# Attention stage: projections of two sequences one slot later, a tile's sum ahead of the next tile's gathers, statistics between row maxima

## The reference

```python
x = layernorm(x + ssm(x))             # state-space mixer
x = layernorm(x + moe(x))             # 64 experts, 8 per token, and a shared one
x = layernorm(x + attention(x))       # 16 heads of 8, per sequence
x = layernorm(x + mlp(x))             # three layers of +1/-1 weights
```

```python
q = split_heads(x @ Wq.T + bq)
k = split_heads(x @ Wk.T + bk)
v = split_heads(x @ Wv.T + bv)
scores = einsum('hbnd,hbmd->hbnm', k, q) * SCALE
attn = softmax(scores, axis=-1)
out = einsum('hbnm,hbmd->hbnd', attn, v)
```

## Time and profile before

| | us |
|---|---|
| three runs, median (lowest to highest) | 871.92 (866.49 to 875.07) |
| the profiled execution | 876.69 |
| its span, first to last instruction | 874.9 |
| mean granted TensorE clock | 0.85 of full speed |
| PE busy | 618.2 (71%) |
| DVE busy | 483.3 (55%) |
| ACT busy | 400.1 (46%) |
| POOL busy | 365.7 (42%) |

### The profile page before, as it was taken

How to read it: one execution, slowest core, us unless ns; L and a number is a source line. 1 busy time by engine, 2 the same in 40 slices (tenths; PEclk the granted TensorE clock), 3 DMA queues, 4 the chain that set the end, 5 groups by cost and what they waited for, 6 DMA issues and landing times.

```text
span 874.9 us, 13107 instructions
## 1 busy us (share of the span) xinstructions
PE 618.2 (71%) x3680; PEld 385.2 (44%) x3713; DVE 483.3 (55%) x1238; ACT 400.1 (46%) x900; POOL 365.7 (42%) x401
## 2 busy tenths in 40 slices
PE   4872109600179999930978977877978999998995
PEld 2451006300158999920968863222222233343443
DVE  4870015300036655600645677686866887867986
ACT  4420103200024666600534648555756777787651
POOL 4157750677720000075032433787477070013552
PEclk9876558855579999965879997898989999999999
DMA  8999410211102666631545645242241131000001
GB/s 270 373 247 344 169 42 1 87 54 51 48 1 72 178 172 171 180 88 42 159 119 145 166 126 150 62 138 56 52 127 54 29 104 56 1 2 0 2 12 37
DMA packets 99628, 91.52 MB, mean 105 GB/s; under 512 B 10784, under 2 KB 84608, under 8 KB 98688
## 3 DMA queue, kind: packets, MB, share of 16 engines
q1 hardware_dynamic: 90704, 75.01, 28.6%
q0 software_dynamic: 7680, 15.74, 6.2%
q10 hardware_dynamic: 1200, 0.23, 0.1%
HBM read 45.14 MB, written 45.61 MB: 104 GB/s over the span
## 4 chain that ended last, share of the span: by engine, by line
PE 46%; another core or an unknown queue 18%; DVE 14%; issue 12%; ACT 6%; DMA 2%; POOL 1%; ACTq 1%; SPq 0%; POOLq 0%; DVEq 0%
PE ps L1621 7%; PE ps L1608 6%; PE ps L1726 5%; PE ps L1736 5%; PE ps L1716 4%; DVE mx L1230 4%; PE ps L1631 3%; PE ps L1616 3%; PE ps L1530 2%; PE ps L1535 2%; ACT big L807 2%; DVE arena L1348 1%; ACT arena L773 1%; DMA dmat_s<-dmat 1%
## 5 line engine op out<-in xcount | busy, mean ns | idle before, releaser
L1230 DVE TENSOR_REDUCE mx<-ps 128x2 f32<-128x1024 f32 x128 | 151.0, 1217 | 49.5 <-PE ps L1716 37.9
L807 ACT ACTIVATE big<-ps 128x512 f32<-128x512 f32 x256 | 141.4, 598 | 67.2 <-PE ps L1726 32.7
L558 POOL DMA_INDIRECT big<-od,idx x72 | 69.0, 958 | 187.2 <-DMA od<-big 123.6
L542 POOL DMA_INDIRECT xd<-xt,idx x120 | 116.2, 968 | 69.7 <-issue 35.7
L1535 PE MATMUL ps<-arena,hmT 96*128 96x128 f32 x128 | 26.9, 343 | 125.8 <-issue 102.1
L1152 DVE TENSOR_TENSOR hm<-sg,ps 128x176 f32<-128x176 f32 x124 | 41.7, 336 | 118.1 <-ACT sg L745 74.1
L1621 PE MATMUL ps<-arena,xbT 128*128 x496 | 99.8, 325 | 4.7 <-DVE xbT L1156 2.7
L1726 PE MATMUL ps<-arena 128*128 128x512 bf16 (+1 forms) x234 | 82.6, 395 | 24.4 <-ACT big L807 11.6
L1608 PE MATMUL ps<-arena,hmT 96*128 x496 | 80.4, 286 | 26.4 <-issue 22.4
L1535 PEld LDWEIGHTS ps<-arena,hmT 96*128 96x128 f32 x128 | 21.0, 229 | 142.2 <-issue 108.0
L735 ACT ACTIVATE big<-ps 128x256 f32<-128x256 f32 x124 | 47.7, 384 | 76.2 <-PE ps L1608 47.0
(11 more groups left out here) (221 smaller groups left out, 1088.7 us busy)
## 6 DMA issues: line engine op xcount, KB each, us to landing
big<-xd SPq DMA_DIRECT2D x62, 256.0 KB
od<-big SPq DMA_DIRECT2D x62, 256.0 KB
arena<-scr SPq DMA_DIRECT2D x96, 96.0 KB
xd<-zeros SPq DMA_DIRECT2D x1, 8192.0 KB
xd<-zeros SPq DMA_DIRECT2D x1, 7680.0 KB, 30.9
arena<-w_gu SPq DMA_DIRECT2D x4, 1408.0 KB, 21.3
arena<-w_d SPq DMA_DIRECT2D x4, 768.0 KB, 17.7
scr<-places SPq DMA_DIRECT2D x8, 384.0 KB
```

The lines of the kernel that those rows point to most:

```text
L542: pool.indirect_dma_start(out=xd[f], out_offset=bass.IndirectOffsetOnAxis(ap=idx[:, t, k:k + 1], axis=0), in_=xt[:, t], in_offset=None).th ...
L558: pool.indirect_dma_start(out=slot[:, k], out_offset=None, in_=od[f], in_offset=bass.IndirectOffsetOnAxis(ap=idx[:, t, k:k + 1], axis=0)). ...
L807: act.activation(ering[:, HG * (mt % 2) + h], ps[:, 4 + h % 2, :], ACT.Exp, scale=SCALE).then_inc(exp_ready, 1)
L1230: v.tensor_reduce(mx[:, k, TB * h + 2 * a:TB * h + 2 * a + 2], ps[:, 2 * a:2 * a + 2, :], AX_X, ALU.max).then_inc(s1_free, 1)
```

## The change

Sequence 1 stays as it was. For sequence 2 (and 3):

- x goes from slot 0 to slot 1 of group 4 (8), q from slot 1 to slot 2, k from slot 2 to slot 0 of group 5 (9), v from slot 0 to slot 1 of that group.
- The normalisation comes behind the third maximum of group 4 (fourth of group 8), the v bias behind the seventh maximum of group 5 (9). DVE's split steps of sequence 2 have places of their own: q behind the seventh and eighth maximum of group 4 and the first of group 5, k behind the fourth, fifth and sixth of group 5.
- The statistics of sequence 3 go from the end of group 7 to behind the second maximum of group 8; those of sequence 2 stay at the end of group 3.
- SP writes the keys of sequences 2 and 3 behind the maxima's DMA and not in front of it.
- POOL sums tile 11 ahead of tile 12's gathers, and makes the root of sequence 2 behind four gathers of tile 12 and not behind two of tile 13.

```diff
--- before.py
+++ after.py
@@ -75,12 +75,15 @@
 
 
     LATER = {(0, 0): ("x", 1), (0, 1): ("q", 1), (0, 2): ("k", 1), (1, 0): ("v", 1),
-             (4, 0): ("x", 2), (4, 1): ("q", 2), (4, 2): ("k", 2), (5, 0): ("v", 2),
-             (8, 0): ("x", 3), (8, 1): ("q", 3), (8, 2): ("k", 3), (9, 0): ("v", 3)}
+             (4, 1): ("x", 2), (4, 2): ("q", 2), (5, 0): ("k", 2), (5, 1): ("v", 2),
+             (8, 1): ("x", 3), (8, 2): ("q", 3), (9, 0): ("k", 3), (9, 1): ("v", 3)}
     SLOTS = ((1, 2), (2, 2), (3, 0))
-    STATS_IN = {4: 2, 8: 3}
-    TURN_IN = {i: b for (i, _), (what, b) in LATER.items() if what == "x"}
-    PARTS_AT = ((0, 2, 1), (0, 3, 0), (0, 3, 1), (0, 3, 1), (1, 0, 0), (1, 0, 1))
+    STATS_AT = {(3, HG - 1, 1): 2, (8, 0, 1): 3}
+    NORM_AT = {(4, 1, 0): 2, (8, 1, 1): 3}
+    V_AT = {(1, 2, 0): 1, (5, 3, 0): 2, (9, 3, 0): 3}
+    PARTS_AT = {1: ((0, 2, 1), (0, 3, 0), (0, 3, 1), (0, 3, 1), (1, 0, 0), (1, 0, 1)),
+                2: ((4, 3, 0), (4, 3, 1), (5, 0, 0), (5, 1, 1), (5, 2, 0), (5, 2, 1))}
+    WRITE_KEYS_LATER = (6, 10)
     WRITE_IN = {2: 1, 6: 2, 10: 3}
     HEAD_GROUPS = 10
     LOADS = {0: (2,), 1: (3,), 2: (4, 5), 3: (6,), 4: (7,), 6: (8, 9), 7: (10,), 8: (11,), 10: (12, 13), 11: (14,), 12: (15,)}
@@ -445,12 +448,15 @@
                 if i in WRITE_IN:
                     write_parts(sp, WRITE_IN[i], 0)
                     load_stack(sp, GB * WRITE_IN[i], 0)
-                    write_parts(sp, WRITE_IN[i], 1)
+                    if i not in WRITE_KEYS_LATER:
+                        write_parts(sp, WRITE_IN[i], 1)
                 sp.wait_ge(mT_copied, i + 1)
                 hd = HG * (i % (2 * GB))
                 if i >= 1:
                     sp.wait_ge(max_in, 16 * i)
                 sp.dma_start(kst[KM:P, hd:hd + HG, :].rearrange("p h n -> p (h n)"), mT[:, i % 2, :]).then_inc(max_in, 16)
+                if i in WRITE_KEYS_LATER:
+                    write_parts(sp, WRITE_IN[i], 1)
                 for n in LOADS.get(i, ()):
                     if n % GB:
                         load_stack(sp, n, 0)
@@ -594,11 +600,14 @@
             bring(1, FIRST[1], back_slot(FIRST[1]))
             rstd_of(2 * B + 1)
             for t in range(FIRST[1] + 1, NT):
-                bring(1, t, back_slot(t), 0, 2)
-                if t == 3 * TB + 1:
+                if t == 3 * TB:
+                    sum_rows(t - 1)
+                bring(1, t, back_slot(t), 0, 4)
+                if t == 3 * TB:
                     rstd_of(2 * B + 2)
-                bring(1, t, back_slot(t), 2, TOP_K)
-                sum_rows(t - 1)
+                bring(1, t, back_slot(t), 4, TOP_K)
+                if t != 3 * TB:
+                    sum_rows(t - 1)
             sum_rows(NT - 1)
 
             def qk_parts(b):
@@ -1266,6 +1275,11 @@
                     v.wait_ge(s_r, 3 * i + 3)
                     v.tensor_tensor(mp[:, k, 2], r, mp[:, k, 1], ALU.subtract).then_inc(split_done, 1)
 
+            def late_stats(b):
+
+                v.wait_ge(summed, TB * (b + 1) - MINE - DENSE)
+                stats(tmp, B + b)
+
             def dve_group(i, k):
                 ahead = not isinstance(i, int) or i + 2 < NGR
                 after = not isinstance(i, int) or i + 1 < NGR
@@ -1276,23 +1290,24 @@
                         if after and h == 0 and a == 1:
                             copy_max(i + 1, 1 - k)
                         if isinstance(i, int):
-                            if (h, a) == (0, 1) and i in TURN_IN and i:
-                                normalise(xt, tmp, 2 * B + TURN_IN[i])
-                            if (h, a) == (2, 0) and LATER.get((i, 0), ("", 0))[0] == "v":
-                                v_in(LATER[i, 0][1], 7)
-                            for b, i0 in ((1, 0), (2, 4)):
-                                for n, place in enumerate(PARTS_AT):
-                                    if place == (i - i0, h, a):
+                            if (i, h, a) in NORM_AT:
+                                normalise(xt, tmp, 2 * B + NORM_AT[i, h, a])
+                            if (i, h, a) in V_AT:
+                                v_in(V_AT[i, h, a], 7)
+                            for b in PARTS_AT:
+                                for n, place in enumerate(PARTS_AT[b]):
+                                    if place == (i, h, a):
                                         qk_part(b, n // 3, n % 3)
+                            if (i, h, a) in STATS_AT and (h, a) != (HG - 1, 1):
+                                late_stats(STATS_AT[i, h, a])
                 out = not isinstance(i, int) or i >= 1
                 for step in range(4):
                     if ahead:
                         split_max(i + 2, k, step)
                     if out and step < 2:
                         norm_out(i - 1, 1 - k, step)
-                if isinstance(i, int) and i + 1 in STATS_IN:
-                    v.wait_ge(summed, TB * (STATS_IN[i + 1] + 1) - MINE - DENSE)
-                    stats(tmp, B + STATS_IN[i + 1])
+                if isinstance(i, int) and (i, HG - 1, 1) in STATS_AT:
+                    late_stats(STATS_AT[i, HG - 1, 1])
 
             for h in range(HG):
                 for a in range(2):
@@ -1310,7 +1325,7 @@
                         stats(tmp, B + 1)
             for step in range(4):
                 split_max(1, 1, step)
-            normalise(xt, tmp, 2 * B + TURN_IN[0])
+            normalise(xt, tmp, 2 * B + 1)
             for i in range(HEAD_GROUPS):
                 dve_group(i, i % 2)
             with v.Fori(HEAD_GROUPS // 2, NGR // 2 - 1) as j:
@@ -1835,7 +1850,7 @@
             def later_sequence(i, slot):
 
                 what, b = LATER.get((i, slot), ("", 0))
-                if what and slot == 0:
+                if what and not any((i, earlier) in LATER for earlier in range(slot)):
                     pe.wait_ge(mT_copied, i + 2)
                 if what == "x":
                     turn_in(b, ps[:, 7, :])
```

## The result

| | before | after |
|---|---|---|
| median of 13 runs, us (lowest to highest) | 870.89 (865.03 to 875.57) | 876.17 (868.0 to 878.46) |
| ratio after / before, 95% interval | | 1.0075 (1.005 to 1.0099) |
| profiled execution; its span | 876.69; 874.9 | 876.17; 874.4 |

The changed kernel is slower by 0.75%, about 6.5 us. The two profiled executions are alike by accident: in this one the mark of group 2 comes 7.4 us earlier (587.50 against 594.88), from stretches that the change doesn't touch, and by the mark of group 10 (720.01 against 720.49) nearly all of it is given back. So the loss is read between these two marks: 125.6 us before, 132.5 after, +6.9. It is the difference of one execution of each, and single groups vary: groups 0 and 1, which the change doesn't touch, take 21.54 and 19.21 us in the one, 16.33 and 22.50 in the other.

A forecast was written before the change was run, and what follows sets the result against it. PE was taken as the floor, with idle gaps and low clock above it. Group 2 -2.0, group 4 -2.3, group 5 -0.5, group 6 -1.0, group 8 -2.3, group 9 +4.0 make -4.1: 867.8 us, range 858 to 878.

The forecast's parts named there:

- Part 1, group 2: Group 2: with tile 11 summed first, tile 12's gathers leave the loads of stack 6 and a long quarter shortens, -2 us.
- Part 1, its price: GpSimd enters its statistics wait six gathers behind, 7.3 us less 2; its 12.59 us of idle time hides that.
- Part 2: Groups 4 and 8: moving x, q, k and v of sequences 2 and 3 gains 2.3 us each.
- The bias wait: Last quarter of groups 5 and 9: the later v bias addition costs 0.8 us each, at most 2.
- Part 3: Key path after moving k: group 9 with the opening of 10 +4.0 us, group 5 -0.5, group 6 -1.0.
- late keys would be covered there by gaps: Groups 5 and 6: remaining gaps hide the late keys of sequence 2, the argument against the slower end, +12 us.
- B: Openings of groups 6 and 10: PE stands for late keys, then runs at the low clock; +12, 884 us; chance 0.13.
- A: Attention groups: gaps go as gathers and stack loads part, and keys come in time; -13, 859 us; chance 0.20.
- C: Attention groups: gaps only move and the projections' gain is given back at once; 872 us; chance 0.20.
- D: DVE's q and key splits blocked beside GpSimd's sums, group 6 opening 2.6 us later; -1, 871 us; chance 0.07.

## Why the prediction was wrong

The change was forecast at -4.1 us and measured at +6.5. Two terms of the sum failed: the price of the postponed gathers, put at nothing, and the projections and keys in groups 4 to 6.

**Part 1, group 2: right in size** (-2 forecast, -2.95 measured), but probably not for the reason given. I had the gathers leave the loads of stack 6. In the kernel before, those loads were issued from 597.23 to 599.65; in the long quarter from 603.08 on the DMA engines are busy 0.2 of the time and from 607 not at all, where it was 0.76 between 599 and 601. The quarter is long at the end of a row of eight gathers, and group 2 of the changed kernel has only four. That all three kernels with the early sum have 12.4 to 13.8 us there on this kind of chip, against 16.70 in one execution of the kernel before, agrees with it; on the second kind the earlier sum gains nothing in group 2.

**Part 1, its price: the step that failed.** I wrote of POOL's six postponed gathers that POOL's idle time in front of the statistics of sequence 3 "hides it", which took their cost as lateness of POOL alone. That half held on the chip of the comparison: POOL idled 15.81 us there in place of 12.59 (it was ahead by more, where I had said by less). But the gathers went into group 4, whose term I then took as -2.3 from the projections alone. It came out at +5.4, which is 7.7 of the 11.0 us between the forecast (-4.1) and what the two traces show (+6.9). With the gathers moved and the projections as before it was +4.6. The rows were there: the earlier trace rows are gaps late in a run of eight gathers. I had read them as gathers together with stack loads, because group 4, with six gathers and no stack load, had a small idle part; its six showed none. The longer run shows gaps with no stack load beside it.

**Part 2.** Group 8 -1.8 for -2.3: right. The bias wait is 1.47 us for 0.8, in both groups, within its bounds. For group 4 the term of -2.3 is found only on the second kind, at -1.7 with GpSimd's new order (17.16 to 15.46) and -2.7 with the old. On the first kind it was lost in the gaps: group 4 is 0.8 us longer than with the gathers alone.

**Part 3.** Group 9 with the opening of 10: +3.8 for +4.0, and PE does wait for SP at both openings. The sum is right partly by luck: the bias is 1.47 for 0.8, the stack is 0.59 late for 2.1 (12.4 us from k's matmul for 13), and PE's busy time grows by 1.6 for 1.1. For sequence 2 the stack is ready 16.0 us after k's matmul, for 14.8. Groups 5 and 6: +1.2 and +1.05 for -0.5 and -1.0, 3.8 us off together. The claim that late keys would be covered there by gaps is half true: on the second kind, where there are no gaps, the same moves cost +6.3 and +1.8.

**The rivals.** B (the slower end) named the keys, and said that the kernel is slower once its waits cost over 6.2 us; in the comparison the four waits (two for the bias, two for stacks) make 5.0, and group 4 is no part of B. Where no gap covers them the keys and the bias decide, with +8.1 us in groups 5 and 6. A and C are out: the time rose, clear of noise. Of D, a key split of sequence 2 took 1.77 us beside a sum's multiply of 646.49:

```profile
646.49 1.91 POOL L576 TENSOR_TENSOR arena<-arena,wk 128x1024 f32<-128x1024 f32 x1
647.19 1.77 DVE L1201 TENSOR_TENSOR places<-ra,places 128x512 bf16<-128x512 f32 x1
```

One such place, not three; the same step takes 0.68 us at 636.17. The row agrees with the rule of the Trainium skill that D rested on ("SBUF — State Buffer", section "SBUF: two separate sides"), of a DVE operation with two SBUF inputs that is blocked by a GpSimd one reading SBUF; the price is 1.1 us here.

**What stays open.** Why DVE and ACT stand beside rows of gathers on one kind of chip and not on the other, and what decides where in a row: the waits until "remote" open behind the third gather at the earliest (ACT from 643.89, in a row begun at 640.34), mostly behind the fifth or later, and one row of eight of the kernel before (from 563.09) has none. That the engines stand there is read from the traces of four executions. That the gathers are the cause is argued from where the waits lie, and the count rests on these traces alone.

## What to carry to other kernels

When instructions are postponed behind a wait, price them twice: as lateness of their own engine, and as load on whatever runs beside them where they land. A small gap in one place is no proof that a cause is absent there; look at how much of the suspect that place had. And a transfer with few us of lead (the keys) should not be moved to gain a slot: sequence 3's moves gave 1.8 us and cost 3.8 in the comparison, and much the same on the other kind of chip.

## What the runs showed of the hardware

The same program took 870 us on one kind of chip and 655 to 658 on the other (medians). On the first kind ScalarE's waits beside scatters and gathers reach 16.5 us and groups 2 and 6 take 16.70 and 17.41 us; on the second both take 12.12, the floor. The gathers themselves are issued every 1.25 us on both. A schedule tuned on one kind is tuned to its gaps: the change makes group 4 longer by 5.4 us on the first and shorter by 6.2 on the second.
